# Three copies of the token sums instead of two, in a mixture-of-experts kernel with gated long convolution

## What is computed

```python
x = x + tanh(g_xattn[0]) * xattn(ctx_2048, ctx_2048, layernorm(x), ssm_kernel, D, 8)
# ffn of layernorm(x):  T = 16*128 = 2048 tokens, E = 32, TOPK = 6
combine = zeros((T, E)).at[arange(T)[:, None], topk_idx].add(topk_w)
eo = einsum('etm,emh->eth', silu(g) * u, down_w)       # every expert's output
routed = einsum('te,eth->th', combine, eo)             # sum over a token's 6 experts
shared = silu(xf @ sh_gate_w) * (xf @ sh_up_w) @ sh_down_w
x = x + tanh(g_ffn[0]) * (routed + shared)
```

## Time and profile before

| | us |
|---|---|
| median of three runs | 584.55 |
| lowest and highest | 584.04, 584.76 |
| the profiled execution | 584.76 |
| its span (first to last instruction) | 582.7 |
| busy in the span: PE, DVE, POOL, ACT | 444.6, 309.3, 298.3, 200.4 |
| mean granted TensorE clock | 0.884 |

### The profile page before, as it was taken

One profiled execution on the slowest core, in us unless ns is written; L12 is line 12 of the kernel. 1 busy time (PEld: TensorE's weight loads), 2 busy tenths in 40 slices (PEclk: granted clock), 3 DMA queues, 4 the chain that ended last, 5 costly groups with the idle time before them and its releaser, 6 DMA issues.

```text
span 582.7 us, 8574 instructions
## 1 busy us (share of the span) xinstructions
PE 444.6 (76%) x2098; PEld 335.0 (57%) x2098; DVE 309.3 (53%) x1137; ACT 200.4 (34%) x506; POOL 298.3 (51%) x240
## 2 busy tenths in 40 slices
PE   0272798789889668700699999999999999999900
PEld 0262676567766446400477777777777777777700
DVE  3789969966995724400344444444444444444306
ACT  2150633633553331100144444444444444444400
POOL 2600008875884750077065666666666666666630
PEclk9995789979979957855699999999999999999955
DMA  6999002222221588575256666666666666565559
GB/s 261 354 322 428 2 1 94 96 93 69 91 101 71 179 377 236 137 225 179 82 108 109 108 115 115 116 115 113 112 113 111 115 114 118 108 115 108 76 115 356
DMA packets 52953, 85.35 MB, mean 146 GB/s; under 512 B 6460, under 2 KB 47644, under 8 KB 52252
## 3 DMA queue, kind: packets, MB, share of 16 engines
q0 software_dynamic: 20160, 28.37, 25.4%
q1 hardware_dynamic: 32398, 45.00, 24.8%
q10 hardware_dynamic: 342, 11.35, 6.2%
HBM read 44.91 MB, written 39.80 MB: 145 GB/s over the span
## 4 chain that ended last, share of the span: by engine, by line
PE 65%; DVE 12%; issue 10%; DMA 6%; ACT 2%; POOL 2%; SPq 1%; DVEq 0%; POOLq 0%; ACTq 0%
PE bank L1052 21%; PE bank L1071 15%; PE bank L941 6%; PE bank L912 5%; DVE arena L603 4%; PE bank L1043 4%; PE bank L1062 4%; PE bank L962 3%; DMA token_sums<-work,dest 3%; PE bank L913 2%; DMA arena<-toeplitz 2%; PE bank L983 2%; PE bank L932 1%; DVE arena L613 1%; DMA arena<-token_sums 1%
## 5 line engine op out<-in xcount | busy, mean ns | idle before, releaser
L383 POOL DMA_INDIRECT token_sums<-work,dest x108 | 168.4, 1559 | 116.1 <-DMA token_sums<-work,dest 47.8
L1052 PE MATMUL bank<-wgu,work 128*128 x432 | 146.8, 462 | 0.0
L1071 PE MATMUL bank<-wd,work 88*128 x432 | 111.0, 379 | 0.0
L369 POOL DMA_INDIRECT expert_lists<-arena,slots x48 | 59.8, 1246 | 83.2 <-DVE slots L703 69.2
L865 DVE TENSOR_TENSOR work<-work,bank 128x176 f32<-128x176 f32 x108 | 36.5, 338 | 120.1 <-ACT work L507 119.0
L1052 PEld LDWEIGHTS bank<-wgu,work 128*128 128x128 f32 x432 | 74.1, 191 | 23.2 <-issue 0.5
L507 ACT ACTIVATE work<-bank 128x176 f32<-128x176 f32 x108 | 34.3, 318 | 143.8 <-PE bank L1052 136.4
L369 POOL DMA_INDIRECT expert_lists<-payload,slots x48 | 56.6, 1179 | 52.1 <-DMA expert_lists<-arena,slots 31.8
L847 DVE COPY work<-bank 128x256 f32<-128x256 f32 x108 | 45.9, 425 | 60.7 <-PE bank L1043 48.7
L1071 PEld LDWEIGHTS bank<-wd,work 88*128 88x128 f32 x432 | 73.3, 190 | 6.1 <-issue 0.2
L1043 PE MATMUL bank<-ident,payload 128*128 128x128 f32 x216 | 42.3, 277 | 36.4 <-DMA payload<-expert_lists 36.4
(11 more groups left out here) (136 smaller groups left out, 478.9 us busy)
## 6 DMA issues: line engine op xcount, KB each, us to landing
payload<-expert_lists SPq DMA_DIRECT2D x108, 144.5 KB
wgu<-w_gu ACTq DMA_DIRECT2D x1, 6688.0 KB
expert_lists<-blank SPq DMA_DIRECT2D x1, 4768.5 KB, 24.6
wgu<-w_gu SPq DMA_DIRECT2D x1, 4576.0 KB, 18.7
arena<-token_sums SPq DMA_DIRECT2D x8, 512.0 KB, 7.4
wd<-w_down ACTq DMA_DIRECT2D x1, 2992.0 KB
token_sums<-blank SPq DMA_DIRECT2D x1, 2304.0 KB, 28.7
arena<-toeplitz SPq DMA_DIRECT2D x1, 2048.0 KB, 11.7
```

Source lines behind the costliest of these rows:

```text
L369: nc.gpsimd.indirect_dma_start(lists, bass.IndirectOffsetOnAxis(ap=slots[:, g % 2, b, k:k + 1], axis=0), pay[g % 2][:, b, :], None).then_i ...
L383: nc.gpsimd.indirect_dma_start(sums, bass.IndirectOffsetOnAxis(ap=dest[:, t % NPICK:t % NPICK + 1], axis=0), y_row(t), None, compute_op=AL ...
L1052: last = nc.tensor.matmul(bank[2 + t % 2][:, 0:2 * M], xT_half(t, k), wgu[:, bass.ds(e * WGU_E + k * 2 * M, 2 * M)], start=(k == 0), stop= ...
L1071: last = nc.tensor.matmul(bank[6 + t % 2][:, 0:L], hT_half(t, c), wd[:, bass.ds(e * WD_E + c * L, L)], start=(c == 0), stop=(c == 1))
```

## The change

S goes from 2 to 3: three copies of `sums`, and an add waits for the add three tiles back. The fill at L263, the loads at L308 and the placement of the results in `arena` follow from S. DVE's final loop gets a second addition with a wait of its own.

```diff
-S = 2
+S = 3
@@
             for c in range(NG):
-                a, b = (win(arena, (S * c + i) * GB * L, [[1, GB * L]]) for i in range(S))
+                a, b, d = (win(arena, (S * c + i) * GB * L, [[1, GB * L]]) for i in range(S))
                 dve.wait_ge(sums_in[c], 16 * S)
                 nc.vector.tensor_tensor(a, a, b, ALU.add).then_inc(f_added, 1)
-                dve.wait_ge(f_added, c + 1)
+                dve.wait_ge(f_added, 2 * c + 1)
+                nc.vector.tensor_tensor(a, a, d, ALU.add).then_inc(f_added, 1)
+                dve.wait_ge(f_added, 2 * c + 2)
                 nc.vector.scalar_tensor_tensor(a, a, gates[:, 1:2],
```

## The result

| | us |
|---|---|
| before, median of 13 runs | 584.04 |
| changed, median of 13 runs | 587.53 |
| ratio, 95% interval | 1.0059 [1.0044, 1.0075] |
| the profiled execution, its span | 592.33, 590.2 |

The change costs 3.5 us (interval 2.6 to 4.4); 4.0 were forecast, 588.5 against a measured 587.53, inside the range. One execution of the kernel before, among those beside e9 to e11, took 1218.5 us and is left out of their ratios. The profiled execution is 4.8 us above the median of its kernel, so its span must not be set against that of before.

The account below looks back on a forecast made before the run. PE's matmuls were taken to bound the tile stage, then POOL's last adds and the DMA engines the end. Gain, loads, addition and fill, −2.6 + 5.3 + 1.3 + 0 = +4.0 us, gave 588.5 us, range 587.1 to 590.3.

Parts of the forecast that it names:

- Where the gain lies: POOL's adds gain only in the tail; in the tile stage PE never waits, so nothing is won there.
- Size of the gain, 2.63: Tail on POOL: with three adds in flight the last add starts 2.63 us earlier, bounds 1.4 to 2.7.
- rival A: Tail adds: a third in flight only lengthens the landings; gain 0 to 1.4 us, 589.8 to 591.2, chance 0.14.
- Loads, 5.3: Reading back the sums: four more 512 KB loads at 1.33 us each cost 5.3 us, limited by the DMA engines.
- One addition exposed, 1.26: DVE's final loop: of four extra additions three lie under the loads, only the last group's costs, 1.26 us.
- the whole end: Reading back and summing three copies after the last add: loads 5.3 plus addition 1.3, cost 6.6 us.
- The fill, 0: Zero fill at L263 grows, moving the last fill 5.2 us later, but is covered, so it costs 0.
- The bound of 8.5: Last fill, L265: lands at most 8.5 us later, at the 261 GB/s of the slowest early slice.
- Rival B: End: DVE and loads overlap better, DVE the bound; cost 5.0 to 5.9 us, 586.9 to 587.8, chance 0.10.
- Rivals C and D: C: POOL's tail gives back nearly all, 585.3, chance 0.04; D: ACT's first rows wait for the fill, 593.7, 0.02.

Follow-up runs that it names:

- e9: Kernel before (two copies, four groups) with copy 1's loads issued by ACT instead of SP; ratio 0.9987, −0.8 us.
- e11: The changed kernel run once more with a second trace, against the kernel before; ratio 1.0064, +3.7 us.
- e2: Changed kernel with three adds in flight but only two copies read back and summed; against the kernel before 0.9957, −2.5 us.
- e7: Kernel before with its end cut into eight groups of two batches instead of four of four; ratio 1.0021, +1.2 us.
- e4: Changed kernel without DVE's second addition and its wait, all 12 loads kept; against the kernel before 1.0056, +3.2 us.
- e1: Kernel before with only the zero fill at L263 enlarged to 4480 KB, two copies used; ratio 0.9999, 0.0 us.
- e5: Changed kernel with DVE's second addition but only 8 loads, copy 1 added again; against the kernel before 1.0045, +2.6 us.

## Why the prediction was right, point by point

- **Where the gain lies.** Right: nothing in the tile stage, PE 259.00 of 259.00 us; only the lag at the end moved. From its first matmul to its last the tile stage takes 271.3 to 272.7 us with three or four adds in flight and 271.1 to 272.8 with two.
- **Size of the gain, 2.63.** Right for the pair of traces (2.67) and for e2 (2.5). But what it was subtracted from is one execution's lag, and six traces with two adds in flight give 1.0 to 4.8. That their mean, 2.6, lies where one trace had it is in part luck: five of the six lie at 2.7 or below, and only e7's 4.8 lifts the mean. The weak step was to take one execution's rows for the kernel's.
- **No longer landing (rival A).** Nearly right. The last add took 3.78 to 4.09 us to land in the seven traces with three or four in flight and 3.62 to 3.80 in the six with two, so 0.2 us more on the mean (3.9 against 3.7), within the 0.4 that the prediction allowed. The Trainium skill ("DMA: Bandwidth & Descriptors", section "Latency and other measured facts"), with up to 2 us for an access under high load, would have allowed an estimated 1.8 us more; the traces show 0.2, at a DMA share of 0.58 in the changed kernel's.
- **Loads, 5.3.** Measured 5.1 in e4; the step was 1.30 us a load (564.7+4.1 to 583.1, eleven steps) and not 1.33. The 358 GB/s of the Trainium skill ("DMA: Bandwidth & Descriptors", section "Where 436 GB/s comes from") would have made it 5.9; the measured steps are faster, 0.524 MB in 1.30 us, which is 403 GB/s.
- **One addition exposed, 1.26.** Measured 1.2, the difference between the changed kernel and e4. Also right is that the other three lie under the loads with hardly any room: DVE idled 0.24 us ahead of the second group and not at all after. In the kernel before, too, DVE had no idle time once its second group had begun, so there the two limits met already. On the old clock the whole end was forecast at +6.6 and is +6.3.
- **The fill, 0.** Right in its price (e1), wrong by its term: the last fill lands 7.0 to 8.0 us later (e11, e1, changed), not 5.2. The 428 GB/s were the rate of a window in which the weights' load runs; while the fill runs, from 34 to 42 us, it is 286 GB/s in the changed kernel's trace. The bound of 8.5 held.
- **Rival B** is half true, and the total can't tell it from the forecast: 587.53 lies in its 586.9 to 587.8 as well. One of its signs came, DVE without idle time between its groups, from the third group on here and from the second on in e11. The other, steps under 1.27 us a load, did not (1.30), and e4 shows that DVE is not the only bound: without the four additions the end falls by 1.2 us, not by 5.0.
- **Rivals C and D** did not occur.

## What to carry to other kernels

Before one more copy is bought to take a wait away, ask on which stretch that wait reaches the end: here POOL waited for landings all through the tile stage (43 times in the trace of before), and only the waits around the last adds counted, 1.0 to 4.8 us, while every copy must be read back and summed, 6.3 to 6.6 us each. Where two limits meet (the last landing and DVE's last group, within a tenth of a microsecond), removing either alone gives back little, so measure each alone before working on one. And a finer cut of the last stage has to earn more than it adds on every engine: here SP's issuing (0.54 us a load) and DVE's shorter operations (0.69 us for half of 1.22) took all that the earlier start gave.

## What the runs showed that I had not expected

With two adds in flight the lag behind the last row of y varied from 3.49 to 7.25 us between executions (e7 corrected as above), and with three or four it was 2.50 in all of seven traces: the added slack takes the variation away as well. It does so although single landings stretch whatever the number in flight. In each of the eleven experiments' traces the longest took 5.2 to 5.9 us, at medians of 3.8 to 4.0. In e5, with three in flight, the last add but one took 5.7 us, and the last add still started 2.50 us behind its row; in e7, with two, 4.51 us for one add moved the last row of y by 2.3 us.

SP's issue of one fill blocked its queue for 8 to 17 us (L263 for 15.3 us before and 16.6 changed, L265 for 8.1 and 14.9), while the 4.9 MB fill ahead of them took 1.4 us to issue; nothing behind them was due, or that would have been the larger price of the fill.
